# Attention over a graph: rows of h turned by the DMA queue are worked on one part later

## The reference, cut to what matters

```
h = max(layernorm(x), 0)
q = h @ W_q.T + b_q ; k = h @ W_k.T + b_k ; v = h @ W_v.T + b_v
z = (q @ k.T) / sqrt(512) * adj ; z = -10000 where z == 0
out = x + relu(softmax(z, axis=1) @ v)
```

## Time and profile before

| | |
|---|---|
| time, median of 3 runs | 1464.02 us (1463.88 to 1464.1) |
| the profiled execution: its own time | 1463.6 us |
| its span, first to last instruction | 1461.8 us |
| PE busy | 1450.5 us, 99% |
| DVE busy | 1301.5 us, 89% |
| ACT busy | 868.4 us, 59% |
| POOL busy | 44.8 us, 3% |
| mean granted TensorE clock | 1.000 |
| DMA | 307.53 MB, 210 GB/s |

### The profile page before, as it was taken

The page is one execution under the profiler, slowest core; times in us unless marked ns, Lnnn a source line. Parts: engine busy times, 40 slices in busy tenths (PEclk is TensorE's granted clock), DMA queues, the critical chain, the costliest instruction groups (busy, mean ns, idle before and its releaser), DMA issues.

```text
span 1461.8 us, 24720 instructions
## 1 busy us (share of the span) xinstructions
PE 1450.5 (99%) x9414; PEld 924.8 (63%) x9414; DVE 1301.5 (89%) x1597; ACT 868.4 (59%) x1398; POOL 44.8 (3%) x27
## 2 busy tenths in 40 slices
PE   9999999999999999999999999999999999999999
PEld 4455556766666666666666666666666666666555
DVE  7979888898999899998989898989898999987986
ACT  4666666765656566655665565656566566655542
POOL 0000000000000000100010001000000001000100
PEclk9999999999999999999999999999999999999999
DMA  6587666374555665566556664666557655665252
GB/s 209 163 269 216 216 183 242 137 298 185 223 216 226 217 238 216 222 217 242 203 204 246 229 229 183 227 245 238 190 224 245 234 186 203 245 217 178 89 163 97
DMA packets 100533, 307.53 MB, mean 210 GB/s; under 512 B 33856, under 2 KB 34112, under 8 KB 98624
## 3 DMA queue, kind: packets, MB, share of 16 engines
q1 hardware_dynamic: 100416, 305.96, 58.4%
HBM read 260.84 MB, written 38.80 MB: 205 GB/s over the span
## 4 chain that ended last, share of the span: by engine, by line
PE 93%; DVE 4%; ACT 1%; issue 1%; DMA 0%; SPq 0%; POOL 0%; DVEq 0%; ACTq 0%
PE o L687 45%; PE za L629 22%; PE zd L629 11%; PE zb L629 5%; PE o L616 4%; PE o L595 3%; PE zb L687 1%; DVE stats L1116 1%; PE za L698 0%; DVE g_buf L1196 0%; DMA slots<-in_L_gnn_W_q 0%; ACT g_buf L838 0%; DVE slots L1290 0%; DVE half_min L1152 0%; DVE slots L1168 0%
## 5 line engine op out<-in xcount | busy, mean ns | idle before, releaser
L687 PE MATMUL o<-v_buf,p_buf 128*128 128x512 f16 x3072 | 726.4, 376 | 0.8 <-DVE p_buf L1322 0.6
L687 PEld LDWEIGHTS o<-v_buf,p_buf 128*128 128x128 f16 x3072 | 300.4, 98 | 260.9 <-issue 1.5
L629 PE MATMUL za<-h_buf,g_buf 128*128 128x256 f16 x2952 | 402.2, 273 | 1.4 <-ACT um_tmp L887 0.7
L629 PEld LDWEIGHTS za<-h_buf,g_buf 128*128 128x128 f16 x2952 | 287.3, 98 | 139.8 <-DVE g_buf L1196 3.5
L629 PE MATMUL zd<-h_buf,g_buf 128*128 128x256 f16 x1476 | 201.3, 273 | 0.0
L907 ACT ACTIVATE slots<-slots,log_p 128x1024 f32<-128x1024 f32 x128 | 146.0, 1141 | 51.4 <-DVE slots L1315 51.4
L1322 DVE TENSOR_TENSOR p_buf<-slots,p_buf 128x1024 f16<-128x1024 f32 x128 | 157.3, 1229 | 14.5 <-PE zb L687 13.6
L1315 DVE TENSOR_TENSOR slots<-slots,floor_b 128x1024 f32<-128x1024 f32 x128 | 169.9, 1329 | 0.3 <-POOL floor_b L547 0.3
L1278 DVE TENSOR_TENSOR slots<-um_tmp,dm_tmp 128x512 f32<-128x512 f32 x128 | 89.1, 696 | 78.7 <-ACT dm_tmp L892 78.7
L902 ACT ACTIVATE slots<-za,c_all,kappa 128x256 f32<-128x256 f32 x128 | 72.2, 564 | 142.4 <-PE za L629 141.5
L1290 DVE SCALAR_TENSOR_TENSOR slots<-slots 128x1024 f32<-128x1024 f32 x128 | 155.9, 1218 | 0.2
(11 more groups left out here) (155 smaller groups left out, 1123.3 us busy)
## 6 DMA issues: line engine op xcount, KB each, us to landing
g_buf<-g_dram SPq DMA_DIRECT2D x108, 896.0 KB, 5.4
v_buf<-v_dram SPq DMA_DIRECT2D x128, 512.0 KB, 3.5
adj_own<-in_adj SPq DMA_DIRECT2D x92, 512.0 KB, 6.2
spare<-in_adj SPq DMA_DIRECT2D x36, 512.0 KB, 6.3
g_dram<-g_buf SPq DMA_DIRECT2D x12, 896.0 KB, 5.5
v_dram<-v_buf SPq DMA_DIRECT2D x16, 512.0 KB, 4.8
spare<-in_x SPq DMA_DIRECT2D x15, 512.0 KB, 7.4
h_buf<-h_dram SPq DMA_DIRECT2D x7, 1024.0 KB, 9.1
```

The lines of the kernel that those rows point to most:

```text
L629: mm = pe.matmul(bank[:, 0:QH], g_of(i)[:, a, op, j, :], right[b][j], start=(fresh and j == 0 and m == 0), stop=(j == 1 and m == 2), skip_ ...
L687: mm = pe.matmul(bank, a[:, kt, span], v_buf[:, n % V_BUFS, kt, b, c:d], start=(j == 0 and kt == 0 and m == 0), stop=(j == PAIRS - 1 and k ...
```

## The change

A function `row_tile(k)` says which tile part k casts, subtracts and multiplies: k+4 for parts 0 to 3 (tiles 4 to 7), none in part 4, k+3 from part 5 on (tile 8 in part 5, tile 31 in part 28). Part k normalises the tile of part k+1. The bias terms of quad 1 stay in part 3, those of quads 2 to 7 go from the end of part 4g-1 to the end of part 4g. In the SP queue the turns of a group move accordingly: tile 4g+3 goes to the very front of group g, ahead of the store of quad g (for g of 2 and more); tile 4g+5 goes behind the store of v, next to 4g+6; tile 4g+4 stays.

```diff
--- before.py
+++ after.py
@@ -329,6 +329,11 @@
 
             return 16 * ((t - TURNED) // ROW_BUFS + 1)
 
+        def row_tile(k):
+
+            t = k + QUAD if k < QUAD else k + QUAD - 1
+            return t if k != QUAD and t < TILES else -1
+
         def opening_pair(k):
 
             g, i = k // QUAD, k % QUAD
@@ -467,6 +472,8 @@
             load_adj(0)
             load_adj(1)
             for g in range(QUADS + 1):
+                if 2 <= g < QUADS:
+                    turn_h(QUAD * g + 3)
                 if 1 <= g < QUADS:
                     store_h(g)
                 if g == QUADS - 1:
@@ -480,15 +487,13 @@
                     load_adj(2 * g - 3)
                 if 1 <= g < QUADS - 1:
                     turn_h(QUAD * g + QUAD)
-                    turn_h(QUAD * g + QUAD + 1)
                 if g < QUADS:
                     store_v(2 * g)
                 if 1 <= g < QUADS - 1:
+                    turn_h(QUAD * g + QUAD + 1)
                     turn_h(QUAD * g + QUAD + 2)
                 if g + 3 < QUADS:
                     load_x(g + 3)
-                if 1 <= g < QUADS - 1:
-                    turn_h(QUAD * g + QUAD + 3)
                 if 2 <= 2 * g - 2 < PAIRS:
                     load_adj(2 * g - 2)
             store_g(PAIRS - 2)
@@ -988,13 +993,13 @@
                         high_g(g - 2, 1)
                 if i == 3 and late_quad(g - 1) and g <= QUADS:
                     high_g(g - 1, 1)
-                if g + 1 < QUADS:
-                    high_h(k + QUAD)
+                if row_tile(k) >= 0:
+                    high_h(row_tile(k))
                 if k in (5, 6):
                     high_t(0, 2 * (k - 5))
                     high_t(0, 2 * (k - 5) + 1)
-                if k + QUAD + 1 < TILES:
-                    normalise(k + QUAD + 1)
+                if row_tile(k + 1) >= 0:
+                    normalise(row_tile(k + 1))
                 if k == 2:
                     square_root(2)
                     for d in range(KC):
@@ -1464,8 +1469,8 @@
                     low_g(g - 1, 0)
                 if i == 0 and 2 <= g <= QUADS + 1 and not late_quad(g - 2):
                     low_g(g - 2, 1)
-                if g + 1 < QUADS:
-                    low_h(k + QUAD)
+                if row_tile(k) >= 0:
+                    low_h(row_tile(k))
                 if k == LATE:
                     low_v(v_tile(k))
                 elif half >= 0:
@@ -1478,8 +1483,8 @@
                     magnitude(1)
                     v.tensor_scalar(kappa[:, :], up_inv[1][:, :], SCALE / UNIT, None, ALU.mult).then_inc(kappa_ready, 1)
                     link(v.tensor_scalar(u_cols[:, :], u_cols[:, :], up[1][:, 0:1], None, ALU.mult))
-                if k + QUAD < TILES:
-                    row_dot(k + QUAD)
+                if row_tile(k) >= 0:
+                    row_dot(row_tile(k))
                 if whole >= 0:
                     negate(whole)
                 if seen_pair >= 0:
@@ -1513,8 +1518,10 @@
                     for t in range(QUAD):
                         aggregate(QUAD * (g + 2) + t)
                     quad_var(g + 2)
-                if i == 3 and g + 1 < QUADS:
-                    key_terms(g + 1)
+                if k == QUAD - 1:
+                    key_terms(1)
+                if i == 0 and 2 <= g < QUADS:
+                    key_terms(g)
 
             late = PAIRS - 2
             add_c11(late)
```

## The result

The changed kernel takes 1468.77 us (median of 7 runs, 1468.62 to 1470.57), the kernel before 1464.02 us (7 runs): 4.75 us more, ratio 1.0037, 95% interval 1.0027 to 1.0047. Forecast were 1469.3 us and a range of 1467.0 to 1472.0. The profiled execution of the changed kernel took 1468.72 us with a span of 1466.9 us, 5.1 us longer than the span before. In the changed file the lines from L332 on stand 5 to 6 lines further down: the load L403 is L408, the first combination L1232 is L1237, and so on.

What follows compares the result with a forecast made beforehand. PE was taken to bound the kernel from 297 us on, so only the opening's delay counts. 5.4 us for the late load less 0.15 for bias terms gave +5.25 us: 1469.3 us, range 1467.0 to 1472.0.

Steps and rivals of the forecast that it cites:

- What bounds: PE is busy 1161.10 of 1165 us from 297 us on; whatever it is late there, the kernel is late at its end.
- The load of block 1: SP queue: h's load issued at 229.29, landing at 237.9; DVE waits 6.0 us at L1232, PE ends 5.4 us late.
- the tied piece: PE's piece of scores at 245.81, 0.64 us of cover after ACT's copy: 5.4 us late, including 3.5 at the earlier piece.
- Part 4 and the bias terms: DVE: part 4's lost tile becomes idle time, 0 (bounds 0 to -1.4 us); quad 2's bias terms leaving part 7, -0.15 us.
- The rival in which the relief of part 4 reaches PE: DVE's freed 1.4 us shorten PE's waits at 64.46 and 72.81, 1.55 us with bias terms: 1462.5 us; chance 0.04.
- The shift: From part 5 on, ACT and DVE do the same instructions on the tile before: cost 0.
- the turns: Three turns per quad go out one part later on SP; the latest keeps 5.6 us of cover before PE: cost 0.
- SP's order: Tile 4g+3's turn ahead of quad g's store delays v, g and adj DMAs, read over a part later: cost 0.
- part 28: DVE gains tile 31's work, at most 1.6 us, covered by its 1.71 us wait before 228.88: cost 0.
- the rival of a late tile: A turn behind packed stores takes over 14 us, PE waits in five quads: +1 to +5 us, 1472; chance 0.04.
- The clock: Rival: after a 3.5 us wait PE returns at 1.2 GHz, not 2.4: +2.7 us, 1472; chance 0.10.
- The quick landing: Rival: in an empty queue the load takes about 6.2 us, freeing DVE at 235.5: term 3.0 us, 1466.9; chance 0.07.

Runs made afterwards that it cites:

- experiment 1: Changed kernel with the load of block 1 of h put ahead of tile 31's turn and quad 7's store in the SP queue: 1463.76 us.
- experiment 2: Changed kernel with DVE's four combinations of T of block 1 each one part later, the load left late: 1463.61 us.
- experiment 3: Kernel before, only the load of block 1 of h issued later, behind both stores of g and the load of adj: 1469.25 us.
- experiment 5: Changed kernel with h's block 1 load ahead of tile 31's turn, and row statistics of tiles 14 and 15 moved from part 5 to 4: 1462.59 us.
- experiment 9: Changed kernel with 15 extra matmuls, no part of the result, filling PE's wait near 240 us: 1469.08 us.
- experiment 8: Changed kernel with the load of block 1 of h and the store of quad 7 exchanged, load directly behind tile 31's turn: 1464.47 us.
- experiment 4: Kernel before, only the load of block 1 of h one place later, behind the store of v, ahead of g's stores: 1464.05 us.
- experiment 7: Kernel before, only the load of block 1 of h behind the two stores of g, ahead of the load of adj: 1466.81 us.

## Why the prediction was right

*What bounds.* Right. The main stage is as long as before, and what PE is late at its start (302.31 against 297.20 at the first L687, forecast 302.5) is what the kernel is late.

*The load of block 1.* Right in place, cause and size. Issue at 229.29, forecast 229.29. Landing at 237.5, forecast 237.9; its 8.2 us lie between the two durations of 7.9 and 9.1 that I had. The cover at the tied piece came out as forecast: 5.66 - 5.03 = 0.63 us. That the forecast is 0.5 us above the measured median comes mostly from the landing, 0.4 us earlier than assumed. DVE starts the combination 5.66 us later (6.0), PE's first piece 3.25 us later (3.5), the tied piece 5.03 us later (5.4). Experiments 1 and 2 take the loss away, one at the load and one at its reader, and experiment 3 makes it without the shift.

*Part 4 and the bias terms.* Right. DVE's idle time before v of tile 5 grew from 0.43 to 1.64 us, and PE's wait at the first scores shrank from 0.42 to 0.29 us, the 0.13 of the bias terms (0.15 forecast). DVE and PE after, the answer to the earlier trace rows:

```profile
53.37 0.69 DVE L1181 TENSOR_TENSOR v_buf<-o,v_buf 128x512 f16<-128x512 f32 x1 [1.64 <-ACT v_buf L820]
...
72.83 0.83 PE L634 MATMUL za<-h_buf,g_buf 128*128 128x256 f16 x6 [0.29 <-DVE g_buf L1201]
```

In this execution the start, where PE waits for the weights, was 0.14 us longer, so at 73 us both kernels stand level; over the profiled executions here of both kernels and their variants, the first quarter of g starts anywhere from 47.08 to 47.76 us. The rival in which the relief of part 4 reaches PE is refuted as it stood: PE's wait at 64 us is still 1.31 us. Experiment 5 shows what the room is worth once other work is put there.

*The shift, the turns, SP's order, part 28.* Right as no cost, by experiment 1 in sum; they weren't taken apart further. PE waits for no turned tile in the trace after, and its slowest turn took 9.7 us to land (9.1 before), short of the 14 us that the rival of a late tile needed. Part 28 took 1.35 us of DVE's idle time, 1.6 forecast.

*The clock.* The rival's condition came true, its price didn't. Busy time in stretches of 2 us after PE's wait (columns as in the earlier trace rows; the granted clock is the third number from the right):

```profile
242.00:244.00 2.00, 0.33 (x3) 0.31 (x4) 2.00 (x3) 2.00 (x6) 0.00 (x0) 1.00 1.01 413
244.00:246.00 2.00, 1.91 (x11) 1.08 (x8) 1.80 (x4) 0.88 (x2) 0.00 (x0) 0.56 0.28 113
246.00:248.00 2.00, 1.71 (x10) 1.30 (x11) 2.00 (x4) 0.60 (x2) 0.00 (x0) 0.59 0.02 2
248.00:250.00 2.00, 2.00 (x13) 1.02 (x12) 1.97 (x4) 1.50 (x2) 0.00 (x0) 1.00 0.82 260
```

From 244.2 to 247.6 us the clock was at 1.2 instead of 2.4 GHz, and six matmuls of 256 columns took 1.49 us instead of 0.82. The Trainium skill, "TensorE: Matmul & The Clock Gate", Part 1, says that idle time brings the clock back to half, and the trace agrees: the fall came 0.5 us after the end of PE's idle 3.07 us, and in experiment 9, where PE has matmuls in that time, the clock stays at 1.000. But I had charged the slow work in full. At full speed PE would have waited 1.14 and 0.44 us for ACT's copies, as it does in experiment 9, because ACT itself waits for DVE (1.90 us before 248.50). The slow work replaced these waits.

Two of the seven runs took 1470.13 and 1470.57 us, 1.4 and 1.8 us over the median, with a mean clock of 0.998 against 0.999 or 1.000 in the others. That a longer time at the low clock explains them isn't shown. Of the four runs of experiment 3 the one at 0.998 took 1469.17 us, less than two of those at 0.999, and the kernel before has three runs of 1465.56 to 1465.67 us at 0.999, 1.8 to 1.9 us over its medians, though its trace has no such long wait of PE.

*The quick landing.* I weighed the 6.15 us for 1 MB of the Trainium skill, "DMA: Bandwidth & Descriptors", section Bandwidth, against rows of 7.9 to 9.3 us and went by the rows. For the change the rows were the right price: with 1 MB of the store issued 0.4 us ahead of it the load landed 8.2 us after its issue. The page's figure is near what the load took without that store just ahead: 6.1 us in experiment 1 and 6.7 in 3, each behind 512 KB of adj issued less than 1 us before, and 5.9 in 8. The Trainium skill's figure is for the transfer alone, while the rows run from the issue to the landing and hold what was queued. So "an empty queue" was the wrong condition for the changed kernel, since the store of quad 7 goes out in it right ahead of the load.

## What to carry to other kernels

When a step moves, look in each queue not only for the step's own reader but for what stands behind it and waits with it: here the whole loss came through a load that has nothing to do with the moved tile and only stood behind it (experiment 1). For each such DMA compare its landing with the start of its first reader; that difference is what the move may use up (3.1 us here; 2 us of it were used in experiment 4 at no cost). Beyond it DVE, which works in order, passed on all but 0.4 to 0.8 us of its wait. And the work taken from DVE ahead of its next wait for another engine was worth nothing here, until other work was moved into the room (experiment 5).

## What was not expected

The time from issue to landing of the same 1 MB load went from 5.9 to 10.6 us with its place in the queue: 5.9 (experiment 8), 6.1 (1), 6.7 (3), 7.8 (7), 8.2 (the change), 9.1 (before), 10.6 (4). It was longest with adj, 1 MB of h and 512 KB of v ahead of it (4), and shortest where only a turn was issued just ahead. A DMA issued 11 us later (3 against before) landed only 8.9 us later.

The clock was still at 1.00 throughout PE's idle 3.07 us in the changed kernel and fell after PE had gone on. In experiment 7 DVE waited 3.22 us, but PE idled in shorter pieces (0.72, 1.15 and 0.44 us) and the clock stayed at 1.0.
